# Two transformer layers on one core: probabilities become the stationary operand of the product with V

## The chip, the core and the metric

The kernel runs on 1 core of one Trainium2 chip. The metric is device time in microseconds (us) of one execution. The engines that matter are TensorE (PE; its weight loads are shown apart as PEld), VectorE (DVE), ScalarE (ACT), GpSimd (POOL) and the DMA queue of SyncE (SP). A matmul on TensorE loads a stationary operand (the weights, one column per output row) and then streams the moving operand through it, column by column, into PSUM. An fp32 product is issued as two passes, each with a load and a matmul, so the trace has two of each.

## What is computed

Two transformer layers over x of 16 batches x 128 tokens x 144 channels, both with 16 heads of 9 channels and a shift and scale taken from a condition; the first has a mixture of 4 experts as its MLP, the second a plain MLP of 576. The part that matters here is the same in both layers:

```python
attn = jax.nn.softmax(jnp.einsum('bhqd,bhkd->bhqk', q, k) * hd ** (-0.5), axis=-1)
o = jnp.einsum('bhqk,bhkd->bhqd', attn, v).transpose(0, 2, 1, 3).reshape(B, N, C)
o = o @ w_proj + b_proj
x = x + g_msa[:, None, :] * o
```

## The kernel before

Everything stays in SBUF between the stages; Q and K go once through a scratch in DRAM to be laid out by head. The order of the whole program is a generator, `program()`, whose steps every engine walks through, each issuing its own part; semaphores join them. Per layer there are 16 batches of 2 pairs; a *pair* here is a half of a batch's heads, 8 of 16. `attention_step(L, p)` emits the steps of pair p:

- `MAX` of pair p + 4 (`scores`, L1348, 8 bf16 matmuls into `s_pair`; VectorE then takes the row maxima, L1096, 1.22 us each), and for the first pair of a batch `MAX_T`, which turns the maxima of the next batch around (L1408) and stores them by a DMA as two extra rows of Q.
- `SCORE` of pair p (`scores_T`, L1370, 8 bf16 matmuls into `st_pair`, keys on partitions); ScalarE takes the exponential into `pr` (L824, 1.03 us). `pr` holds two pairs, keys on partitions, 128 queries per head, not normalised.
- `PROJ` of batch b - 2 in even pairs: two fp32 products (L1422, L1423), then VectorE adds the residual.
- `OUT_T` of batch b - 1 in odd pairs, see below.
- steps for the next group of four batches (normalising, transposing, QK and V products, splitting into bf16 parts, loads of Q and K), laid out over the pairs by `prep_order`.
- `PV` of pair p - 1 (`weigh`, L1389), and in odd pairs `ATT_T` of batch b - 1 (two transpositions of `an`, L1414 and L1415, then a copy to `aT`, L837).

The product with V has V as its stationary operand: for a head, 128 keys x 10 columns (9 channels and a column of ones, which gives the sum of the probabilities), and the head's 128 x 128 of `pr` streams. The result of head i lies on 10 partitions from 32 x (i mod 4), so four heads share the array by columns. It stands with channels on partitions, so it has to be turned: ScalarE copies a bank of 128 x 512 to `osb` (`o_out`, L831), TensorE transposes it in four pieces back into the bank (`out_T`, L1399), and then `normalise` on VectorE takes the reciprocal of the sums (L1111) and multiplies (L1114) into `an`. Banks 4 and 5 take turns by batch.

Of the kernel before, what the change touches and what calls it, by code (L numbers as in the profile page):

```python
# [12 lines left out]
P = 128  # L13
BATCH, SEQ, C = 16, 128, 144
HEADS, HD = 16, 9
# [30 lines left out]
def build(nc, x, cond, w_adaln, b_adaln, w_qkv, b_qkv, w_proj, b_proj, w_gate, w1, b1, w2, b2,  # L46
# [7 lines left out]
    with ExitStack() as ctx:  # L54
        def sb(name, shape, dt=F32):
            return ctx.enter_context(nc.sbuf_tensor(name, shape, dt))

        def sem(name):
# [108 lines left out]
        mT = sb("mT", [2 * HEADS, SEQ], BF16)  # L167
        pr = sb("pr", [P, 2, HP * SEQ])
        neg_one = pr[0:2, 0, 0:SEQ // 2].bitcast(BF16)
        osb = sb("osb", [P, 512])  # L170
        wp32, wr32 = resid[:, 0:2 * C], osb[:, 0:2 * C]
        first_resid = (resid, osb, pr[:, 1, 0:GT])
        later_resid = (resid, hid[:, 2 * HQ:2 * HQ + GT], hid[:, 2 * HQ + GT:2 * HQ + 2 * GT])
        rinv = sb("rinv", [P, HEADS])
        an = sb("an", [P, 2 * P])
# [21 lines left out]
            zeroed pooled neg_st silu cond_T cond_c mod_mm mod_T mod_done gate_c gate_st wsplit qk_weights split_s  # L197
            stats_s sums_s vars_s aggr_s rstd_s normed T_done h_main h_hi h_rest r_hi h_ready
            qk_mm part_a part_r part_b part_c scr_w v_mm v_ready
            padded s_mm max_s msplit mt_mm mt_c m_ld st_mm exp_s pv_mm o_ev o_T rinv_s an_s a_T a_c  # L200
            proj_mm att_t x_att g_att_ld0 g_att_ld1 g_mlp_ld gate_x cw_b mix_s mod_read
            gl_mm gl_c lg_T gate_s gate_e cw_s b2_s w1_mm gelu w2_mm acc_s acc_g x_mlp
            f1_mm f1_gelu f2_mm f2_t st_out""".split()
# [78 lines left out]
        def attention_step(L, p):  # L282

            B0, P0 = BATCH * L, NP * L
            b, h = p // PAIRS, p % PAIRS
            pre, first, mid, late = prep_order(L, p)
            yield from pre
            if p + LEAD < NP:
                yield "MAX", P0 + p + LEAD
            if h == 0 and 0 <= b + 1 < BATCH:  # L290
                yield "MAX_T", B0 + b + 1
            if 0 <= p:
                yield "SCORE", P0 + p
            yield from mid
            if h == 0 and 0 <= b - 2:
                yield "PROJ", B0 + b - 2
            if h == 1 and 0 <= b - 1:
                yield "OUT_T", B0 + b - 1
            yield from first
            yield from late  # L300
            if 0 <= p - 1:
                yield "PV", P0 + p - 1
            if h == 1 and 0 <= b - 1:
                yield "ATT_T", B0 + b - 1

        def attention_end(L):

            B1 = BATCH * (L + 1)
            yield "PV", NP * (L + 1) - 1
            yield "PROJ", B1 - 2  # L310
            yield "UP_PE", (L, 0, 2)
            yield "OUT_T", B1 - 1
            yield "GELU", (L, 0, 0)
            yield "UP_PE", (L, 0, 3)
            yield "ATT_T", B1 - 1
            yield "GELU", (L, 0, 1)
            yield "UP_PE", (L, 0, 4)
            yield "GELU", (L, 0, 2)
            yield "PROJ", B1 - 1
            yield "GELU", (L, 0, 3)  # L320
            yield "GELU", (L, 0, 4)
# [428 lines left out]
        def _(act):  # L750
# [72 lines left out]
                    act.wait_ge(s["part_c"], 3 * NG * (Pn // NP) + 6)  # L823
                sc.activation(pr[:, Pn % 2, :], st_pair[:, :], ACT.Exp, scale=SCALE).then_inc(s["exp_s"], 1)  # L824

            def o_out(B):
                need(act, "pv_mm", PAIRS * (B + 1))
                need(act, "o_T", B)
                if B % BATCH == 0:
                    act.wait_ge(s["part_c"], 3 * NG * (B // BATCH) + 6)  # L830
                sc.copy(osb[:, :], bank[O_BANK[B % 2]][:, :]).then_inc(s["o_ev"], 1)  # L831

            def a_out(B):
                o_bank = bank[O_BANK[B % 2]]
                need(act, "a_T", B + 1)
# [71 lines left out]
            for what, i in program():  # L907
                if what == "QK":
                    part_a(*i, QK_BANK[i[0]][i[1]])
                if what == "PART_B":  # L910
                    part_b(*i)
                if what == "V":
                    v_out(*i, V_BANK[i[0] % NG][i[1]])
                if what == "H_MAIN":
                    h_main(i)
                if what == "H_REST":
                    h_rest(i)
                if what == "H_SPLIT":
                    h_round(i)
                    rest_round(i)  # L920
                if what == "MAX_T":
                    m_out(i)
                if what == "SCORE":
                    exp_pair(i)
                if what == "PV" and i % PAIRS == PAIRS - 1:
                    o_out(i // PAIRS)
                if what == "ATT_T":
                    a_out(i)
                if what == "MOD":
                    mod_out(*i)  # L930
                if what == "ROUND_W":
                    round_weights(i)
                if what in ("UP", "GELU"):
                    gelu(*i)
                if what == "LOGITS":
                    logits_out(i)
                if what == "MIX":
                    act.wait_ge(s["gate_e"], i + 1)
                    sc.activation(ex[:, :, :], dl[:, :, :], ACT.Exp).then_inc(s["gate_x"], 1)
# [3 lines left out]
        def _(dve):  # L943
# [9 lines left out]
            def weights(L):  # L953

                dve.wait_ge(s["ld_qkv%d" % L], NQKV[L])
                need(dve, "part_c", 3 * NG * L)
                need(dve, "o_T", BATCH * L)
                for src, dst in ((sq[L], wp32), (sqr[L], wr32)):
                    sv = src[:, 0:2 * C].rearrange("p (w h d) -> p w d h", w=2, d=HD)
                    for w in range(2):  # L960
# [120 lines left out]
            def part_r(a, t, src):  # L1081
                n = rows(t)
                dve.wait_ge(s["part_a"], 3 * a + t + 1)
                if a % NG == 0 and t > 0:
                    need(dve, *(("o_T", BATCH * (a // NG)) if t == 1 else ("pv_mm", NP * (a // NG))))
                else:
                    need(dve, "part_c", 3 * (a - 1) + t + 1)
                v.tensor_tensor(by_batch(resid_of(a, t), n), by_batch(src, n), parts[0:n, t, :, 0, :],
# [17 lines left out]

            def normalise(B):
                o_bank = bank[O_BANK[B % 2]]
                need(dve, "o_T", B + 1)
                ov = o_bank[:, :].rearrange("p (h w) -> p h w", w=SLOT)  # L1110
                v.reciprocal(rinv[:, :], ov[:, :, HD]).then_inc(s["rinv_s"], 1)  # L1111
                dve.wait_ge(s["rinv_s"], B + 1)
                need(dve, "a_T", B)
# [93 lines left out]
            def setup():  # L1207
# [3 lines left out]
                v.memset(sqr[1][:, :], 0.0).then_inc(s["zeroed"], 1)  # L1211
                v.memset(c_nat[:, C:C + 1], 1.0)
                v.memset(hid4[64:65, :], 1.0)
                for i in O_BANK:
                    v.memset(bank[i], 0.0)
                v.memset(low_slots[:, :], 0.0)
                step(v.memset(mask[:, :], 0.0))
                for k in range(NS):
# [19 lines left out]
            for what, i in program():  # L1238
# [18 lines left out]
                    split_weights(i)  # L1257
                if what == "WEIGHTS":
                    weights(i)
                if what == "OUT_T":  # L1260
                    normalise(i)
                if what == "PROJ":
                    attention_residual(i)
# [13 lines left out]
        def _(pe):  # L1277
# [97 lines left out]
            def weigh(Pn):  # L1375
# [9 lines left out]
                    if B % BATCH == 0:  # L1385
                        need(pe, "part_r", 3 * a + 6)
                for i in range(HP):
                    c, q = i % NS, PAIRS * h + i // NS
                    last = te.matmul(bank[O_BANK[B % 2]][SLOT * c:SLOT * c + OW, q * SEQ:(q + 1) * SEQ],  # L1389
                                     V[:, G * (a % 2) + j, HP * h + i, :], pr[:, Pn % 2, i * SEQ:(i + 1) * SEQ],  # L1390
                                     start=True, stop=True)
                last.then_inc(s["pv_mm"], 1)

            def out_T(B):

                o_bank = bank[O_BANK[B % 2]]
                pe.wait_ge(s["o_ev"], B + 1)
                for q in range(4):
                    last = te.transpose(o_bank[:, q * SEQ:(q + 1) * SEQ], osb[:, q * SEQ:(q + 1) * SEQ],  # L1399
                                        ident[:, :])  # L1400
                last.then_inc(s["o_T"], 1)

            def max_T(B):
                pe.wait_ge(s["msplit"], 2 * B + 2)
# [124 lines left out]
            for what, i in program():  # L1529
# [13 lines left out]
                    scores_T(i)  # L1543
                if what == "PV":
                    weigh(i)
                if what == "OUT_T":
                    out_T(i)
                if what == "ATT_T":
                    att_T(i)
                if what == "PROJ":  # L1550
# [42 lines left out]
```

## Time and profile before

| | |
|---|---|
| median of 3 runs | 507.63 us (505.89 to 512.28) |
| profiled execution | 508.33 us, its span 506.4 us |
| busy, share of the span | PE 436.0 us (86%), PEld 349.7 (69%), DVE 303.4 (60%), ACT 276.4 (55%), POOL 88.9 (18%) |
| mean granted clock of TensorE | 0.926 |
| product with V, L1389 | 1024 passes, 43.8 us busy together |
| transpositions of `osb`, L1399 | 128, 21.5 us busy |
| copy to `osb`, L831 | 32, 589 ns each, 18.9 us |
| chain of work that ended last | PE 51%, DVE 15%, SPq 11%, DMA 10%, ACT 6% |

The profile is of one execution. Busy time of an engine is the union of its instructions; matmuls are pipelined and their ends modelled, so the distance from the start of one group to the start of the next tells more than its length. PEclk is the share of 2.4 GHz that was granted: 1.00 is 2.4 GHz, 0.50 is 1.2 GHz, and a mean between is a mixture of these two. In the first exponential (52.6 us) and the last of the first layer (162.6 us) the first attention has its ends, in those at 352.6 and 452.6 us the second. Between lies the expert MLP, after it the plain one.

### The profile page before, as it was taken

How to read it: one execution, taken by the hardware profiler on the slowest of the kernel's cores; microseconds unless marked ns; L12 is line 12 of the kernel's file. 1: busy time of each engine (PE TensorE's matmuls, PEld its weight loads, DVE VectorE, ACT ScalarE, POOL GpSimd, SP SyncE). 2: the span in 40 equal slices, each digit the busy share in tenths (PEclk: the TensorE clock that was granted, in tenths of full speed). 3: DMA queues.
4: the chain of work that ended last, by engine and by line, in shares of the span. 5: the costliest groups of instructions: out<-in, count | busy, mean ns of one | idle time of the engine just before them, and what ended most of it. 6: DMA issues, size and time to landing. Idle time of an engine off the chain costs nothing.

```text
span 506.4 us, 10608 instructions
## 1 busy us (share of the span) xinstructions
PE 436.0 (86%) x4010; PEld 349.7 (69%) x4010; DVE 303.4 (60%) x891; ACT 276.4 (55%) x523; POOL 88.9 (18%) x112
## 2 busy tenths in 40 slices
PE   4846888888889999999994999998898978888996
PEld 1415656666667779879873997797677767657775
DVE  7766576598874326368433362368777756754651
ACT  4642657776474590381174336613768754856552
POOL 3212001020000053045016200802020200000000
PEclk9877689799797999999998899998789997999999
DMA  7846536445431000000000115202435563210112
GB/s 217 248 133 180 155 97 165 142 129 132 125 91 27 1 1 2 25 0 1 24 1 0 28 44 168 68 0 67 137 99 154 152 152 121 69 31 1 49 48 70
DMA packets 51098, 42.49 MB, mean 84 GB/s; under 512 B 33287, under 2 KB 43454, under 8 KB 51044
## 3 DMA queue, kind: packets, MB, share of 16 engines
q1 hardware_dynamic: 51048, 41.82, 29.6%
q8 instruction: 32, 0.52, 0.4%
q14 instruction: 18, 0.15, 0.1%
HBM read 33.20 MB, written 8.29 MB: 82 GB/s over the span
## 4 chain that ended last, share of the span: by engine, by line
PE 51%; DVE 15%; SPq 11%; DMA 10%; ACT 6%; issue 5%; POOL 2%; DVEq 0%; ACTq 0%; POOLq 0%
PE bank L1507 14%; DVE mx L1096 4%; DMA KA<-qk_scratch 4%; PE s_pair L1348 4%; PE st_pair L1370 3%; SPq L617 3%; PE bank L1389 3%; PE bank L1525 3%; DMA qk_scratch<-parts 2%; PE bank L1293 2%; PE s_pair L1298 2%; PE s_pair L1299 2%; PE s_pair L1300 2%; PE st_pair L1298 2%; PE s_pair L1301 2%
## 5 line engine op out<-in xcount | busy, mean ns | idle before, releaser
L1096 DVE TENSOR_REDUCE mx<-s_pair 128x8 f32<-128x1024 f32 x64 | 78.2, 1221 | 35.9 <-PE s_pair L1348 35.3
L1507 PE MATMUL bank<-w_sb,hid 128*128 128x144 f32 x640 | 80.5, 286 | 0.9 <-DVE aT L1184 0.9
L1507 PEld LDWEIGHTS bank<-w_sb,hid 128*128 128x128 f32 x640 | 79.7, 190 | 1.9 <-DVE aT L1184 1.2
L824 ACT ACTIVATE pr<-st_pair 128x1024 f32<-128x1024 f32 x64 | 65.8, 1028 | 18.8 <-PE st_pair L1370 18.5
L873 ACT ACTIVATE hid<-s_pair 128x512 f32<-128x512 f32 x40 | 23.3, 612 | 51.4 <-PE s_pair L1301 51.4
L697 POOL TENSOR_TENSOR rstd<-var_eps,minus_half 128x4 f32<-128x4 f32 x16 | 16.2, 1012 | 175.8 <-DVE var_eps L1051 175.8
L1348 PE MATMUL s_pair<-KA,QA 81*128 81x128 bf16 x416 | 36.4, 238 | 12.1 <-DMA KA<-qk_scratch 8.1
L1389 PE MATMUL bank<-pr,V 128*10 128x128 f32 x1024 | 43.8, 293 | 0.0
L1348 PEld LDWEIGHTS s_pair<-KA,QA 81*128 81x128 bf16 x416 | 28.4, 107 | 21.5 <-issue 14.8
L1370 PE MATMUL st_pair<-QA,KA 83*128 83x128 bf16 x416 | 36.9, 240 | 5.5 <-DMA QA<-mT 5.2
L719 POOL TENSOR_TENSOR bw<-b_sb,cw 128x576 f32<-128x576 f32 x16 | 19.9, 1245 | 87.0 <-DVE cw L1167 87.0
L1370 PEld LDWEIGHTS st_pair<-QA,KA 83*128 83x128 bf16 x416 | 29.9, 109 | 7.0 <-issue 5.8
L1389 PEld LDWEIGHTS bank<-pr,V 128*10 128x10 f32 x1024 | 22.8, 95 | 16.5 <-issue 9.8
L1062 DVE TENSOR_SCALAR xn<-xs,mean,rstd 128x128 f32<-128x128 f32 x64 | 22.7, 354 | 10.1 <-POOL rstd L697 9.9
L1184 DVE SCALAR_TENSOR_TENSOR aT<-bank,cw,aT 128x144 f32<-128x144 f32 x48 | 17.6, 368 | 17.2 <-PE bank L1507 16.1
L763 ACT ACTIVATE h<-bank,b_main,a_main 128x128 f32<-128x128 f32 x64 | 24.0, 456 | 6.1 <-PE bank L1293 6.0
L837 ACT COPY aT<-bank 128x256 f32<-128x256 f32 x32 | 11.9, 373 | 27.9 <-PE bank L1415 27.8
L1399 PE MATMUL bank<-ident,osb 128*128 128x128 f32 x128 | 21.5, 294 | 4.5 <-ACT osb L831 4.3
L704 POOL TENSOR_TENSOR parts<-resid,parts 32x512 bf16<-32x512 f32 x8 | 9.2, 1150 | 91.9 <-ACT parts L799 91.9
L774 ACT ACTIVATE r<-bank,b_rest,a_rest 128x128 f32<-128x128 f32 x60 | 22.6, 465 | 4.0 <-PE bank L1293 3.9
L794 ACT CAST parts<-bank 128x512 bf16<-128x512 f32 (+1 forms) x18 | 10.4, 578 | 25.7 <-PE bank L1301 25.6
L873 ACT ACTIVATE hid<-st_pair 128x512 f32<-128x512 f32 x32 | 18.8, 611 | 8.2 <-PE st_pair L1301 8.2
(268 smaller groups left out, 947.8 us busy)
## 6 DMA issues: line engine op xcount, KB each, us to landing
QA<-qk_scratch SPq DMA_DIRECT2D x26, 324.0 KB
KA<-qk_scratch SPq DMA_DIRECT2D x78, 108.0 KB
qk_scratch<-parts SPq DMA_DIRECT2D x16, 384.0 KB, 4.0
g_att<-gate_scratch SPq DMA_DIRECT2D x16, 144.0 KB, 3.8
g_mlp<-gate_scratch SPq DMA_DIRECT2D x8, 288.0 KB, 3.5
hid<-qk_scratch SPq DMA_DIRECT2D x6, 324.0 KB
hid<-qk_scratch SPq DMA_DIRECT2D x18, 108.0 KB
hid<-in_L_cond_w SPq DMA_DIRECT2D x1, 1152.0 KB, 9.3
```

What stands on the lines that cost most here:

```text
L763: last = sc.activation(h32[:, j * SEQ:(j + 1) * SEQ], PREP[:, j * SEQ:(j + 1) * SEQ], ACT.Identity, bias=b_main[:, ph, t:t + 1], scale=a_m ...
L774: last = sc.activation(r32[:, j * SEQ:(j + 1) * SEQ], src[:, j * SEQ:(j + 1) * SEQ], ACT.Identity, bias=b_rest[:, ph, t:t + 1], scale=a_re ...
L824: sc.activation(pr[:, Pn % 2, :], st_pair[:, :], ACT.Exp, scale=SCALE).then_inc(s["exp_s"], 1)
L873: sc.activation(hid[:, m * GT:(m + 1) * GT], bank[m % 4][:, :], ACT.Gelu_apprx_tanh).then_inc(s["gelu"], 1)
L1062: v.tensor_scalar(xn[:, j, :], x_[:, 0:CM], mean[:, j:j + 1], rstd[:, j:j + 1], ALU.subtract, ALU.mult)
L1096: v.tensor_reduce(mx[:, HP * h:HP * (h + 1)], s_pair[:, :].rearrange("p (h k) -> p h k", k=SEQ), AX.X, ALU.max).then_inc(s["max_s"], 1)
L1298: te.matmul(dst, lo[:, cols], hhi[:, :], start=True, stop=False)
L1348: last = te.matmul(s_pair[:, i * SEQ:(i + 1) * SEQ], QAs[k][0:SROWS, HP * h + i, :], KAs[k][0:SROWS, HP * h + i, :], start=True, stop=True)
L1370: last = te.matmul(st_pair[:, i * SEQ:(i + 1) * SEQ], KAs[k][0:MROWS, HP * h + i, :], QAs[k][0:MROWS, HP * h + i, :], start=True, stop=True)
L1389: last = te.matmul(bank[O_BANK[B % 2]][SLOT * c:SLOT * c + OW, q * SEQ:(q + 1) * SEQ], V[:, G * (a % 2) + j, HP * h + i, :], pr[:, Pn % 2, ...
L1399: last = te.transpose(o_bank[:, q * SEQ:(q + 1) * SEQ], osb[:, q * SEQ:(q + 1) * SEQ], ident[:, :])
L1507: last = te.matmul(dst, hid[:, at:at + SEQ], w2_sb[:, MT1 * e + i, :], start=(i == 0), stop=(i == MT1 - 1))
```

## The change

In the product with V the operands change places. Stationary is now the head's 128 x 128 of `pr`, and the 10 columns of V stream. The result has queries on partitions and 16 x 10 columns for a batch's heads, as `normalise` wants it, so `o_out` and `out_T` are gone with `osb` and their semaphores. The first residual tile of the split of Q and K, which shared `osb`, is now a tile of its own, `resid1`. `normalise` waits for the product with V itself, and its step, now `NORM`, stands at the start of an odd pair's steps and not after its `PROJ`. Some waits that guarded `osb` go, and so do two memsets of the banks at the start.

```diff
--- before.py
+++ after.py
@@ -167,9 +167,9 @@
         mT = sb("mT", [2 * HEADS, SEQ], BF16)
         pr = sb("pr", [P, 2, HP * SEQ])
         neg_one = pr[0:2, 0, 0:SEQ // 2].bitcast(BF16)
-        osb = sb("osb", [P, 512])
-        wp32, wr32 = resid[:, 0:2 * C], osb[:, 0:2 * C]
-        first_resid = (resid, osb, pr[:, 1, 0:GT])
+        resid1 = sb("resid1", [P, GT])
+        wp32, wr32 = resid[:, 0:2 * C], resid1[:, 0:2 * C]
+        first_resid = (resid, resid1, pr[:, 1, 0:GT])
         later_resid = (resid, hid[:, 2 * HQ:2 * HQ + GT], hid[:, 2 * HQ + GT:2 * HQ + 2 * GT])
         rinv = sb("rinv", [P, HEADS])
         an = sb("an", [P, 2 * P])
...
@@ -285,6 +285,8 @@
             b, h = p // PAIRS, p % PAIRS
             pre, first, mid, late = prep_order(L, p)
             yield from pre
+            if h == 1 and 0 <= b - 1:
+                yield "NORM", B0 + b - 1
             if p + LEAD < NP:
                 yield "MAX", P0 + p + LEAD
             if h == 0 and 0 <= b + 1 < BATCH:
@@ -294,8 +296,6 @@
             yield from mid
             if h == 0 and 0 <= b - 2:
                 yield "PROJ", B0 + b - 2
-            if h == 1 and 0 <= b - 1:
-                yield "OUT_T", B0 + b - 1
             yield from first
             yield from late
             if 0 <= p - 1:
...
@@ -823,13 +823,6 @@
                     act.wait_ge(s["part_c"], 3 * NG * (Pn // NP) + 6)
                 sc.activation(pr[:, Pn % 2, :], st_pair[:, :], ACT.Exp, scale=SCALE).then_inc(s["exp_s"], 1)
 
-            def o_out(B):
-                need(act, "pv_mm", PAIRS * (B + 1))
-                need(act, "o_T", B)
-                if B % BATCH == 0:
-                    act.wait_ge(s["part_c"], 3 * NG * (B // BATCH) + 6)
-                sc.copy(osb[:, :], bank[O_BANK[B % 2]][:, :]).then_inc(s["o_ev"], 1)
-
             def a_out(B):
                 o_bank = bank[O_BANK[B % 2]]
                 need(act, "a_T", B + 1)
...
@@ -1081,8 +1071,8 @@
             def part_r(a, t, src):
                 n = rows(t)
                 dve.wait_ge(s["part_a"], 3 * a + t + 1)
-                if a % NG == 0 and t > 0:
-                    need(dve, *(("o_T", BATCH * (a // NG)) if t == 1 else ("pv_mm", NP * (a // NG))))
+                if a % NG == 0 and t == 2:
+                    need(dve, "pv_mm", NP * (a // NG))
                 else:
                     need(dve, "part_c", 3 * (a - 1) + t + 1)
                 v.tensor_tensor(by_batch(resid_of(a, t), n), by_batch(src, n), parts[0:n, t, :, 0, :],
@@ -1106,8 +1096,8 @@
 
             def normalise(B):
                 o_bank = bank[O_BANK[B % 2]]
-                need(dve, "o_T", B + 1)
-                ov = o_bank[:, :].rearrange("p (h w) -> p h w", w=SLOT)
+                dve.wait_ge(s["pv_mm"], PAIRS * (B + 1))
+                ov = o_bank[:, 0:HEADS * OW].rearrange("p (h w) -> p h w", w=OW)
                 v.reciprocal(rinv[:, :], ov[:, :, HD]).then_inc(s["rinv_s"], 1)
                 dve.wait_ge(s["rinv_s"], B + 1)
                 need(dve, "a_T", B)
@@ -1211,8 +1201,6 @@
                 v.memset(sqr[1][:, :], 0.0).then_inc(s["zeroed"], 1)
                 v.memset(c_nat[:, C:C + 1], 1.0)
                 v.memset(hid4[64:65, :], 1.0)
-                for i in O_BANK:
-                    v.memset(bank[i], 0.0)
                 v.memset(low_slots[:, :], 0.0)
                 step(v.memset(mask[:, :], 0.0))
                 for k in range(NS):
...
@@ -1385,20 +1373,10 @@
                     if B % BATCH == 0:
                         need(pe, "part_r", 3 * a + 6)
                 for i in range(HP):
-                    c, q = i % NS, PAIRS * h + i // NS
-                    last = te.matmul(bank[O_BANK[B % 2]][SLOT * c:SLOT * c + OW, q * SEQ:(q + 1) * SEQ],
-                                     V[:, G * (a % 2) + j, HP * h + i, :], pr[:, Pn % 2, i * SEQ:(i + 1) * SEQ],
-                                     start=True, stop=True)
+                    at = (HP * h + i) * OW
+                    last = te.matmul(bank[O_BANK[B % 2]][:, at:at + OW], pr[:, Pn % 2, i * SEQ:(i + 1) * SEQ],
+                                     V[:, G * (a % 2) + j, HP * h + i, :], start=True, stop=True)
                 last.then_inc(s["pv_mm"], 1)
-
-            def out_T(B):
-
-                o_bank = bank[O_BANK[B % 2]]
-                pe.wait_ge(s["o_ev"], B + 1)
-                for q in range(4):
-                    last = te.transpose(o_bank[:, q * SEQ:(q + 1) * SEQ], osb[:, q * SEQ:(q + 1) * SEQ],
-                                        ident[:, :])
-                last.then_inc(s["o_T"], 1)
 
             def max_T(B):
                 pe.wait_ge(s["msplit"], 2 * B + 2)
```

TensorE, the first whole batch of layer 0 from its second product with V on (`pr` and `V` are the operands of that product, `osb` and `an` those of the transpositions); first before:

```order
L1389 MATMUL bank<-pr,V 10x128 x8
L1348 MATMUL s_pair<-KA,QA 128x128 x8
L1370 MATMUL st_pair<-QA,KA 128x128 x8
L1399 MATMUL bank<-ident,osb 128x128 x4
L1389 MATMUL bank<-pr,V 10x128 x8
L1414 MATMUL bank<-ident,an 128x128
L1415 MATMUL bank<-ident,an 128x128
```

and the same place in the change:

```order
L1377 MATMUL bank<-V,pr 128x10 x8
L1336 MATMUL s_pair<-KA,QA 128x128 x8
L1358 MATMUL st_pair<-QA,KA 128x128 x8
L1377 MATMUL bank<-V,pr 128x10 x8
L1392 MATMUL bank<-ident,an 128x128
L1393 MATMUL bank<-ident,an 128x128
```

The four transpositions are gone; the product is 128 x 10 where it was 10 x 128; nothing else stands elsewhere on this engine.

VectorE at the first row maximum after a batch's product with V (`mx` is the maximum, `mp_pad` its two bf16 parts, `rinv` and `an` the output of `normalise`); first before:

```order
L1096 TENSOR_REDUCE mx<-s_pair 128x8
L1103 CAST mp_pad<-mx 128x16
L1105 TENSOR_TENSOR mp_pad<-mx,mp_pad 128x16
L1111 RECIPROCAL rinv<-bank 128x16
L1114 TENSOR_TENSOR an<-bank,rinv 128x144
L1072 TENSOR_TENSOR hlo<-h,hhi 128x512
```

and in the change:

```order
L1101 RECIPROCAL rinv<-bank 128x16
L1104 TENSOR_TENSOR an<-bank,rinv 128x144
L1086 TENSOR_REDUCE mx<-s_pair 128x8
L1093 CAST mp_pad<-mx 128x16
L1095 TENSOR_TENSOR mp_pad<-mx,mp_pad 128x16
L1062 TENSOR_TENSOR hlo<-h,hhi 128x512
```

The two instructions of `normalise` have moved ahead of the maximum and its split.

## Rows read from the trace of the kernel before

**Rows 1.** The granted clock of TensorE from the page, in 40 slices of the span.

```profile
PEclk9877689799797999999998899998789997999999
```

**Rows 2.** Stretches of both attentions: us, busy (x) per engine, PEclk, DMA share, GB/s.

```profile
52.60:162.60 110.00, 94.29 (x1174) 72.20 (x1172) 80.39 (x191) 72.58 (x133) 9.96 (x9) 0.86 0.44 119
352.60:452.60 100.00, 87.63 (x1178) 68.71 (x1177) 71.89 (x184) 67.14 (x122) 9.95 (x9) 0.91 0.42 119
```

**Rows 3.** Timeline of TensorE in two pairs: start us, us, engine, line, operation [idle before].

```profile
408.87 0.66 PE L1399 MATMUL bank<-ident,osb 128*128 128x128 f32 x4
409.46 0.62 PE L1389 MATMUL bank<-pr,V 128*10 128x128 f32 x16
410.60 0.33 PE L1414 MATMUL bank<-ident,an 128*128 128x128 f32 x1 [0.52 <-DVE an L1114]
...
410.88 0.61 PE L1348 MATMUL s_pair<-KA,QA 81*128 81x128 bf16 x8
...
411.39 0.61 PE L1370 MATMUL st_pair<-hid 83*128 83x128 bf16 x8
411.83 0.46 PE L1422 MATMUL bank<-wo_r,aT 128*128 128x144 f32 x2
...
412.47 0.63 PE L1389 MATMUL bank<-pr,V 128*10 128x128 f32 x16
413.03 0.62 PE L1348 MATMUL s_pair<-KA,QA 81*128 81x128 bf16 x8
```

**Rows 4.** Timeline of the same stretch, ScalarE's exponentials.

```profile
408.85 1.03 ACT L824 ACTIVATE pr<-st_pair 128x1024 f32<-128x1024 f32 x1
...
414.14 1.02 ACT L824 ACTIVATE pr<-st_pair 128x1024 f32<-128x1024 f32 x1 [0.39 <-PE st_pair L1370]
```

**Rows 5.** Weight loads (PEld) and matmuls: timeline rows, then lines with min/median/max ns.

```profile
411.78 0.30 PEld L1422 LDWEIGHTS bank<-wo_r,aT 128*128 128x128 f32 x2
412.47 0.34 PEld L1389 LDWEIGHTS bank<-pr,V 128*10 128x10 f32 x16
...
173.15 0.41 PE L1488 MATMUL bank<-ident,lgT 4*128 4x4 f32 x4
...
233.45 2.72 PE L1507 MATMUL bank<-w_sb,hid 128*128 128x144 f32 x20 [0.94 <-DVE aT L1184]
...
L1507 PEld LDWEIGHTS bank<-w_sb,hid x640: 186/190/192, 187.3 to 346.0; 128*128 128x128 f32 x160
L1507 PE MATMUL bank<-w_sb,hid x640: 283/286/390, 187.5 to 346.1; 128*128 128x144 f32 x160
...
L1488 PE MATMUL bank<-ident,lgT x16: 198/198/220, 173.2 to 309.7; 4*128 4x4 f32 x16
...
L1389 PEld LDWEIGHTS bank<-pr,V x1024: 87/92/143, 55.5 to 455.4; 128*10 128x10 f32 x171
```

**Rows 6.** Timeline of TensorE in a stretch at the lower clock.

```profile
419.07 1.01 PE L1348 MATMUL s_pair<-KA,QA 81*128 81x128 bf16 x8 [2.73 <-DMA KA<-qk_scratch]
...
420.83 0.79 PE L1422 MATMUL bank<-wo_r,aT 128*128 128x144 f32 x2
...
422.03 1.04 PE L1389 MATMUL bank<-pr,V 128*10 128x128 f32 x16
```

**Rows 7.** Two pairs of neighbouring stretches, columns as in Rows 2.

```profile
63.30:66.80 3.50, 2.09 (x25) 1.71 (x24) 2.38 (x4) 1.35 (x4) 0.00 (x0) 0.99 0.60 171
66.80:70.20 3.40, 3.40 (x31) 1.81 (x30) 2.19 (x8) 1.54 (x3) 0.00 (x0) 0.50 0.08 27
414.90:418.30 3.40, 0.64 (x10) 0.20 (x2) 0.84 (x5) 0.64 (x2) 0.00 (x0) 1.00 0.56 164
418.30:425.10 6.80, 6.03 (x55) 5.26 (x56) 3.71 (x8) 2.03 (x4) 0.00 (x0) 0.50 0.53 171
```

**Rows 8.** Timeline of TensorE over one QK product and the group after it.

```profile
102.46 0.48 PE L1298 MATMUL bank<-hhi,wqk_lo 128*128 128x512 f32 x1
...
103.57 0.63 PE L1389 MATMUL bank<-pr,V 128*10 128x128 f32 x16
```

More of the change, by code:

```diff
@@ L199, in build @@
             qk_mm part_a part_r part_b part_c scr_w v_mm v_ready
-            padded s_mm max_s msplit mt_mm mt_c m_ld st_mm exp_s pv_mm o_ev o_T rinv_s an_s a_T a_c
+            padded s_mm max_s msplit mt_mm mt_c m_ld st_mm exp_s pv_mm rinv_s an_s a_T a_c
             proj_mm att_t x_att g_att_ld0 g_att_ld1 g_mlp_ld gate_x cw_b mix_s mod_read
@@ L311, in attention_end @@
             yield "UP_PE", (L, 0, 2)
-            yield "OUT_T", B1 - 1
+            yield "NORM", B1 - 1
             yield "GELU", (L, 0, 0)
@@ L924, in _ @@
                     exp_pair(i)
-                if what == "PV" and i % PAIRS == PAIRS - 1:
-                    o_out(i // PAIRS)
                 if what == "ATT_T":
@@ L956, in weights @@
                 need(dve, "part_c", 3 * NG * L)
-                need(dve, "o_T", BATCH * L)
                 for src, dst in ((sq[L], wp32), (sqr[L], wr32)):
@@ L1259, in _ @@
                     weights(i)
-                if what == "OUT_T":
+                if what == "NORM":
                     normalise(i)
@@ L1545, in _ @@
                     weigh(i)
-                if what == "OUT_T":
-                    out_T(i)
                 if what == "ATT_T":
```

## The prediction

> **What bounds the kernel now.** I read first the stages. The two attention stretches take 110 and 100 us of the 506.4 us span, at a mean granted clock of 0.86 and 0.91 [rows 2]; the clock row of the page is at its lowest in these stretches and full in the expert part between them [rows 1]. Nothing outside them runs a changed instruction except the setup of VectorE, so the sum is made over these 210 us.
>
> Then I read TensorE's timeline in a quiet piece, two pairs of heads of one batch [rows 3]. Each row's distance to the next is what the group really occupies (the rows' lengths include the drain). From 410.88 to 413.03 there is no gap: scores and the small transposition 0.51, transposed scores 0.44, projection 0.64, product with V 0.56. The even pair is bound by TensorE's queue. The odd pair has the four transpositions of `osb` (0.59, 408.87 to 409.46), and then TensorE stands: the product with V is out of its way by about 410.0, the transposition of `an` starts only at 410.60, idle for 0.52 of it, since VectorE normalises after these transpositions. The two pairs together take 5.29 us from exponential to exponential [rows 4]. 32 batches of that are 169 us; the other 41 of the 210 are steps with QK or V products or transpositions for the next group between, waits for the loads of Q and K, and stretches at 1.2 GHz.
>
> **What the change removes.** The copy on ScalarE, the four transpositions (0.59 per batch) and the idle 0.52 behind them go. I count no gain for the copy itself: ScalarE is then waited for by nobody, because TensorE becomes much slower. The memsets of two banks at the start go too; I leave that at nothing (they can only shorten the start). `normalise` moves in VectorE's queue ahead of a row maximum, and now waits for the product with V directly. Queued behind it are that maximum, for which the next scores wait, but the maximum needs scores that stand behind the same product in TensorE's queue, so VectorE would wait anyway: nothing. If that cover were gone it would cost the reciprocal and product, about half a us a batch. No DMA is issued or moved.
>
> **What it adds: the weight loads.** A product of fp32 runs as two passes, each a load and a matmul (1024 for 512 heads). Before, a load has 10 columns and lasts 92 ns; 16 passes occupy 0.56 us with the change of array mode around them [rows 3, 5]. Now each of 16 passes loads 128 columns of fp32 and streams 10. The loads of this form last 190 ns, and the pair of them before the projection takes 0.30, so they follow each other at 0.30 - 0.19 = 0.11 us [rows 5]. Twenty passes of the expert product, 128 columns loaded and 144 streamed, take 2.72, so (2.72 - 0.29)/19 = 0.128 us each; there streaming may be what binds. So a pass costs 0.11 to 0.128; I take 0.115. The group is 16 x 0.115 = 1.84, and 0.10 more because the first load (190 against 92 ns) can't begin before the exponential is there: 1.94 us. The far lower bound is the transposition of logits, 128 columns loaded and 4 streamed: (0.41 - 0.20)/3 = 0.07 us; but it is one pass of another mode. The far upper one is twice 0.11, load and matmul not overlapping at all: 0.22.
>
> *At 2.4 GHz.* One batch: 0.51 + 0.44 + 0.64 for the even pair, 0.45 + 0.45 + 0.28 for the odd one (0.28 is 410.60 to 410.88), 2 x 1.94 for V: 2.77 + 3.88 = 6.65 us against 5.29. No other engine is near that. 32 batches are 213 us. 22 steps carry QK, V or early MLP products, at 1.1 us as between 102.46 and 103.57 [rows 8]; V's are shorter, so 1.0 on average, 22. 12 steps carry four transpositions, 0.5 each, 6. The last four pairs of a layer have no scores, -4. Waits for loads shrink, since a batch gives them 1.4 us more; I leave 5. Sum 242 us, against 210: +32.
>
> *At 1.2 GHz.* Here I expect the larger part. The product with V streamed all 128 columns of the probabilities; now it streams 10 and spends its time loading. Of a batch's 6.65 us, columns stream in about 4 x 0.44 (scores), 0.5 (projection), 0.2 (transpositions) and 0.3: 2.8 us, 41%; before, with 0.4 for the transpositions and 0.8 for V, 3.7 of 5.29, 69%. What the clock does is seen in pairs of stretches [rows 7]. In 63.30 to 66.80 TensorE was busy for 2.09 of 3.5 us, with two waits for DMAs in it, and the next stretch was granted 0.50. In 414.90 to 418.30 it stood for a load, 0.64 busy, and 418.30 to 425.10 ran at 0.50, although TensorE was busy 6.03 of 6.80 there. At 0.50 everything is as slow as the row 420.83 to 422.03 says, 1.20 for the projection that took 0.64 [rows 6]. A TensorE that is the bound and runs at half the clock streams half as many columns a us, which keeps it there: before, it had slack at 2.4 GHz and dense work at 1.2 and came back; now it hasn't. Both layers' attention begins beside such stretches.
>
> The price, with everything doubled: even pair without V 2.96 (419.07 to 422.03 [rows 6]), odd one 2 x 1.18 = 2.36, V 16 x 0.23 + 0.1 = 3.78 each. A batch is 12.9, 32 of them 412; the extra products 2 x 28 = 56; no scores at the end, -7: 461 us, +251, which gives 759. Not all of it will be at 1.2 GHz: the stretch 66.80 to 70.20, at 0.50 itself, had a QK product in it and no wait [rows 7], and the clock must have risen soon after it, since the page's slice 63.3 to 76.0, the sixth, still reads 0.8 [rows 1]. I let half of the 22 steps with such products run at 2.4 GHz, each 12.9/2 + 2.0 - (6.65/2 + 1.0) = 4.1 us shorter: -45. That half is a choice, between none (759) and all attention (540). So 508.3 + 251 - 45 = **714 us**. The profiled execution took 508.3 (span 506.4, the rest lies around it), the median of the runs 507.6, so no correction.
>
> The Trainium skill, TensorE: Matmul & The Clock Gate, section LDWEIGHTS, gives a load as its columns / 1.2 GHz, 107 ns for 128; the 0.11 of the trace agrees. The Trainium skill, TensorEngine Tiling, section Performance Considerations, advises for 32 or fewer moving columns to swap the operands and tile by columns, which is the kernel before: it speaks against this change, as the sum does.
>
> **The rivals.**
> 1. *The clock stays as it is (chance 0.27).* Loads may keep the clock up as streaming does; nothing in before separates them, since where 128 columns are loaded long streams run too. Then +32: 540 us, and 10 more for each 0.01 a pass (64 x 16 x 0.01), to 553 at 0.128.
> 2. *Not slower (0.08).* TensorE's pass costs 0.07, as in the logits' transposition. V is 16 x 0.07 + 0.1 = 1.22, a batch 2.77 + 2.44 = 5.21; in all 32 x 5.21 + 24 = 191, plus 13 of waits for loads that then stay: 204, so -6, 502 us. It decides from 0.07 us a pass downward. If a pass cost what the 10-column loads do, (0.34 - 0.09)/15 = 0.02 [rows 5], V would be 16 x 0.02 + 0.1 = 0.42, a batch 3.6, and VectorE and ScalarE would bind before that: under 498, chance 0.02 of the 0.08. Against both: fp32 loads of 128 columns last 190 ns wherever two passes are made, and follow 0.11 apart. The Trainium skill, TensorE: Matmul & The Clock Gate, section Back-to-back issue gap, has one price, about 25 ns, for any matmul of 1 to 64 columns, without its load; it is on the side of this rival.
> 3. *Slower still (0.07).* Loads overlap nothing, 0.22 a pass: 64 x 16 x 0.105 = 108 us more at 2.4 GHz (648), twice that at 1.2 (over 900).
> 4. *Mostly at 1.2 GHz (0.58)*: my forecast, its own range 650 to 765.
>
> **Numbers.** Range 535 to 765: it leaves out rival 2 and most of rival 3, and holds the rest. About 2% is what a measurement here can tell from no change. Faster by over 2% needs a pass under 0.06: 0.02. Within 2%: 0.06. Slower: 0.92.
>
> **What would show it.** The group of the product with V: 16 loads of 190 ns, 0.11 to 0.12 apart (0.22 to 0.24 at 0.50). No rows of `osb`; `an` ready long before its transposition. ScalarE and VectorE waiting for TensorE in every pair. Granted clock of the attention stretches near 0.5 to 0.6 where it was 0.86 and 0.91; if it is above 0.8, my main step is wrong and the time is near 540. If loads stand 0.07 apart or less, the whole argument falls.

## The result

The changed kernel takes 618.25 us, median of 6 runs (614.86 to 628.92), where the kernel before takes 506.79 (6 runs, 505.57 to 512.28): 1.219 times as long, 95% interval 1.2135 to 1.225. The sign was forecast, and the mechanism; the size was not: 714 us was predicted, 206 us more than before, and 111 came.

The profile is of one execution, the slowest of the six (628.92 us, span 627.1), so it is compared below with the profiled execution of the kernel before (span 506.4), 121 us shorter. Its page, in the rows that answer to those of before: busy time, and the granted clock in 40 slices [rows 1].

```profile
PE 586.0 (93%) x3882; PEld 533.9 (85%) x3882; DVE 302.2 (48%) x889; ACT 260.5 (42%) x491; POOL 89.8 (14%) x112
...
PEclk9866567885555579999997999956969555555999
...
L1377 PEld LDWEIGHTS bank<-V,pr 128*128 128x128 f32 x1024 | 189.6, 282 | 2.7 <-issue 0.5
L1377 PE MATMUL bank<-V,pr 128*128 128x10 f32 x1024 | 184.6, 321 | 0.0
```

The weight loads of the product with V alone fill 189.6 us. The two attentions, again from the first exponential of a layer to its last, by stretches (us, busy of PE, PEld, DVE, ACT, POOL, granted clock, DMA):

```profile
51.20:214.90 163.70, 163.41 (x1119) 159.25 (x1117) 80.68 (x194) 65.37 (x117) 10.83 (x9) 0.60 0.31 81
411.50:565.90 154.40, 154.40 (x1122) 150.99 (x1122) 74.36 (x187) 59.90 (x107) 9.93 (x9) 0.64 0.28 77
```

They were 110 and 100 us at 0.86 and 0.91 [rows 2]; now 163.7 and 154.4 at 0.60 and 0.64. That is 108 of the 121 us between the two profiled executions. Behind both attentions the same low clock runs on, to 228.6 and 580.1 us, and there most of the rest lies. TensorE is busy in 163.41 of the 163.7 us and in all of the 154.4; it is the one bound.

A batch in the part without extra products, timeline of TensorE (start, length, line, operation). It answers to [rows 3]:

```profile
495.94 3.53 PE L1377 MATMUL bank<-V,pr 128*128 128x10 f32 x16
499.32 0.45 PE L1392 MATMUL bank<-ident,an 128*128 128x128 f32 x1
...
499.78 1.06 PE L1336 MATMUL s_pair<-KA,QA 81*128 81x128 bf16 x8
500.63 0.31 PE L1386 MATMUL bank<-identb,mp_pad 128*128 128x128 bf16 x1
500.74 1.06 PE L1358 MATMUL st_pair<-QA,KA 83*128 83x128 bf16 x8
501.59 0.79 PE L1400 MATMUL bank<-wo_r,aT 128*128 128x144 f32 x2
...
502.66 3.43 PE L1377 MATMUL bank<-V,pr 128*128 128x10 f32 x16
505.93 1.01 PE L1336 MATMUL s_pair<-KA,QA 81*128 81x128 bf16 x8
...
507.59 1.61 PE L1377 MATMUL bank<-V,pr 128*128 128x10 f32 x7
```

Not one row waits. From 495.94 to 507.59 is 11.65 us for the batch (the kernel before took 5.29, at 2.4 GHz [rows 4]), 6.65 of them in two groups of the product with V (3.38 and 3.27, at 1.2 GHz). The same group at 2.4 GHz, in a stretch that had it:

```profile
99.03 1.85 PE L1377 MATMUL bank<-V,pr 128*128 128x10 f32 x16
100.74 0.31 PE L1392 MATMUL bank<-ident,an 128*128 128x128 f32 x1
```

1.71 us. A matmul of the group lasts 0.17 at the least, so a pass costs (1.85 - 0.17)/15 = 0.112 us at 2.4 GHz, and (3.43 - 0.37)/15 = 0.204 at 1.2. What the clock did, by stretches:

```profile
51.10:88.60 37.50, 37.21 (x216) 35.12 (x213) 16.00 (x39) 14.73 (x27) 3.31 (x3) 0.50 0.36 94
88.60:102.30 13.70, 13.70 (x154) 13.52 (x155) 8.33 (x19) 7.92 (x17) 1.16 (x1) 1.00 0.65 154
102.30:115.90 13.60, 13.60 (x80) 13.31 (x80) 6.76 (x13) 7.33 (x14) 0.00 (x0) 0.50 0.33 102
115.90:136.40 20.50, 20.50 (x213) 19.73 (x211) 15.92 (x32) 13.21 (x23) 4.35 (x3) 1.00 0.48 115
136.40:228.60 92.20, 92.20 (x516) 90.10 (x516) 34.75 (x98) 25.45 (x44) 2.01 (x2) 0.50 0.16 43
```

Two things are to be seen. The clock is at 1.2 GHz while PE is busy for the whole stretch, and for up to 92 us on end; in the kernel before, both falls shown followed waits [rows 7], and here TensorE ran without a gap through the one at 136.40. And the rise at 88.60 came right behind a QK product, four matmuls that stream 512 columns each (the last two are shown):

```profile
87.44 0.63 PE L1288 MATMUL bank<-hR,wqk_r 128*128 128x512 f32 x1
87.87 0.63 PE L1289 MATMUL bank<-hhi,wqk_hi 128*128 128x512 f32 x1
88.30 2.01 PE L1377 MATMUL bank<-V,pr 128*128 128x10 f32 x16
```

The rises at 115.9, 433.4 and 467.5 us also fall inside or right behind a QK product, the one at 457.2 does not; and behind the QK product that ended at 79.98 the clock stayed down. So such a product goes before most of the rises, but it doesn't always bring one.

### The profile page after: what moved, and what is told of

The parts are those of the page before. It is cut to its first block, busy times and chain, and to the rows that moved or that the text cites. A ratio compares the mean times of both kernels' runs of the same rounds, so it can differ in the third digit from the quotient of the medians.

```text
span 627.1 us, 10304 instructions
## 1 busy us (share of the span) xinstructions
PE 586.0 (93%) x3882; PEld 533.9 (85%) x3882; DVE 302.2 (48%) x889; ACT 260.5 (42%) x491; POOL 89.8 (14%) x112
## 4 chain that ended last, share of the span: by engine, by line
PE 82%; SPq 5%; DVE 3%; ACT 3%; DMA 2%; POOL 2%; issue 1%; DVEq 0%; ACTq 0%; POOLq 0%
PE bank L1377 27%; PE bank L1485 12%; PE st_pair L1358 7%; PE s_pair L1336 6%; PE bank L1400 3%; PE bank L1281 2%; PE bank L1401 2%; PE bank L1503 2%; PE s_pair L1286 2%; PE st_pair L1286 2%; PE s_pair L1287 2%; PE s_pair L1288 2%; PE s_pair L1289 2%; SPq L617 1%; PE st_pair L1287 1%
## 5 line engine op out<-in xcount | busy, mean ns | idle before, releaser
L1377 PEld LDWEIGHTS bank<-V,pr 128*128 128x128 f32 x1024 | 189.6, 282 | 2.7 <-issue 0.5
L1377 PE MATMUL bank<-V,pr 128*128 128x10 f32 x1024 | 184.6, 321 | 0.0
L824 ACT ACTIVATE pr<-st_pair 128x1024 f32<-128x1024 f32 x64 | 65.5, 1024 | 107.7 <-PE st_pair L1358 107.7
L1336 PE MATMUL s_pair<-KA,QA 81*128 81x128 bf16 x416 | 44.0, 270 | 6.6 <-DVE mx L1086 3.5
L1358 PE MATMUL st_pair<-QA,KA 83*128 83x128 bf16 x416 | 47.3, 282 | 2.6 <-DMA QA<-mT 2.3
L1336 PEld LDWEIGHTS s_pair<-KA,QA 81*128 81x128 bf16 x416 | 38.9, 131 | 9.8 <-DVE mx L1086 5.9
L1358 PEld LDWEIGHTS st_pair<-QA,KA 83*128 83x128 bf16 x416 | 39.7, 133 | 3.2 <-issue 2.5
L1114 DVE TENSOR_TENSOR tmp<-bank,g_att 128x144 f32<-128x144 f32 x32 | 9.8, 305 | 63.9 <-PE bank L1401 63.9
L704 POOL TENSOR_TENSOR parts<-resid,parts 32x512 bf16<-32x512 f32 (+1 forms) x12 | 14.1, 1174 | 126.8 <-ACT parts L799 126.8
L1101 DVE RECIPROCAL rinv<-bank 128x16 f32<-128x16 f32 x32 | 8.2, 256 | 45.6 <-PE bank L1377 45.6
L1286 PE MATMUL bank<-hhi,wqk_lo 128*128 128x512 f32 (+1 forms) x18 | 11.2, 622 | 12.4 <-DVE hR L1068 12.4
```

Of the source, the lines that this page charges most:

```text
L1286: te.matmul(dst, lo[:, cols], hhi[:, :], start=True, stop=False)
L1336: last = te.matmul(s_pair[:, i * SEQ:(i + 1) * SEQ], QAs[k][0:SROWS, HP * h + i, :], KAs[k][0:SROWS, HP * h + i, :], start=True, stop=True)
L1358: last = te.matmul(st_pair[:, i * SEQ:(i + 1) * SEQ], KAs[k][0:MROWS, HP * h + i, :], QAs[k][0:MROWS, HP * h + i, :], start=True, stop=True)
L1377: last = te.matmul(bank[O_BANK[B % 2]][:, at:at + OW], pr[:, Pn % 2, i * SEQ:(i + 1) * SEQ], V[:, G * (a % 2) + j, HP * h + i, :], start=T ...
```

## Experiments on the clock

Is the low clock the cost, and do the thin streams cause it? The same loads, in the same places, with more columns streamed beside them tell.

**More columns, 120.**

```diff
-                    last = te.matmul(bank[O_BANK[B % 2]][:, at:at + OW], pr[:, Pn % 2, i * SEQ:(i + 1) * SEQ],
-                                     V[:, G * (a % 2) + j, HP * h + i, :], start=True, stop=True)
+                    dst = bank[O_BANK[B % 2]][:, at:at + 12 * OW].rearrange("p (r w) -> p r w", w=OW)
+                    last = te.matmul(dst, pr[:, Pn % 2, i * SEQ:(i + 1) * SEQ],
+                                     V[:, G * (a % 2) + j, HP * h + i, :].unsqueeze(1).to_broadcast([P, 12, OW]),
+                                     start=True, stop=True)
```

> The changed kernel, but each product with V streams its head's 10 columns twelve times over: 120 columns to the same place and the 110 behind it, which the next heads then overwrite with their own results. The output is the same. Streaming 120 columns of fp32 should take 240 cycles, 0.10 us at 2.4 GHz, and lie beside the next load (0.112 us a pass in the changed kernel). Theory A (the clock falls because TensorE streams too little while it loads): granted clock of the attention stretches back above 0.95, the 16 passes still 1.8 us, time about 540 us. Theory B (the clock falls for another reason, or loads alone count for nothing and nothing else helps): clock 0.62 to 0.66 in attention as before, time 618 us. Theory C (a stream and the next load don't overlap): passes of 0.2 us, time above 618.

Measured: 516.24 us (4 runs, 515.7 to 518.6), 1.0196 times the kernel before, interval 1.0165 to 1.0226. Its attentions, by stretches, and a batch of its timeline:

```profile
53.50:163.40 109.90, 107.67 (x1119) 104.39 (x1117) 79.32 (x194) 65.03 (x118) 10.82 (x9) 0.97 0.45 119
355.00:462.00 107.00, 106.90 (x1122) 104.53 (x1122) 73.66 (x187) 59.90 (x106) 9.92 (x9) 0.98 0.40 111
```

```profile
424.03 2.00 PE L1378 MATMUL bank<-V,pr 128*128 128x120 f32 x16
425.86 0.27 PE L1394 MATMUL bank<-ident,an 128*128 128x128 f32 x1
...
427.04 0.47 PE L1402 MATMUL bank<-wo_r,aT 128*128 128x144 f32 x2
427.34 0.41 PE L1403 MATMUL bank<-wo_m,aT 128*128 128x144 f32 x2
427.58 1.94 PE L1378 MATMUL bank<-V,pr 128*128 128x120 f32 x16
429.36 0.61 PE L1336 MATMUL s_pair<-KA,QA 81*128 81x128 bf16 x8
429.81 0.61 PE L1358 MATMUL st_pair<-QA,KA 83*128 83x128 bf16 x8
430.26 0.99 PE L1378 MATMUL bank<-V,pr 128*128 128x120 f32 x7
```

Twelve times the streaming in this product makes the kernel 102 us faster. It does the same loads; the granted clock of attention is 0.97 and 0.98. The group takes 1.83 and 1.78 us, a little more than 1.71: a stream of 120 columns stays beside the loads. Theory A holds, B and C fall; its time, 540 us, was 24 too high, for the reasons given below. A batch takes 6.23 us (424.03 to 430.26).

**30 and 60 columns**, the same edit with 3 and 6 in place of 12.

> The same with the 10 columns streamed three times over, 30 columns. Theory A: part of the way, attention's granted clock 0.7 to 0.9, 570 to 605 us. Theory B: 618. Theory C: passes 0.02 us longer, 640.

> The changed kernel with the 10 columns of each product streamed six times over, 60 columns. 10 columns gave 618 us, 30 gave 592 to 620, 120 gave 516. Theory A (the clock follows what TensorE streams): the stream of 60 stays hidden beside the load, so passes 0.112 us; granted clock in attention above 0.9, 516 to 535 us. Rival (120 columns helped because TensorE's passes become as long as a load, so that it never stands between them): at 60 half of each pass is still empty, clock and time stay near those of 30 columns, 590 or more.

| columns streamed a pass | time, us | of before | granted clock, first and second attention |
|---|---|---|---|
| 10 (the change) | 618.25 (614.9 to 628.9) | 1.219 | 0.60, 0.64 |
| 30 | 611.66 (591.9 to 619.8) | about 1.21, no interval | 0.69, 0.66 |
| 60 | 531.91 (526.5 to 543.3) | 1.049 (1.039 to 1.059) | 0.86, 0.90 |
| 120 | 516.24 (515.7 to 518.6) | 1.020 (1.017 to 1.023) | 0.97, 0.98 |

The clocks are those of one execution each, from the first exponential of a layer to its last, with 30 columns and then with 60:

```profile
51.50:198.70 147.20, 145.80 (x1120) 142.14 (x1117) 80.45 (x194) 65.15 (x117) 10.88 (x9) 0.69 0.34 90
395.80:547.30 151.50, 151.50 (x1123) 147.82 (x1123) 74.42 (x187) 60.12 (x107) 9.95 (x9) 0.66 0.28 79
```

```profile
50.10:172.50 122.40, 120.20 (x1119) 116.18 (x1120) 82.65 (x195) 64.95 (x117) 10.05 (x9) 0.86 0.42 108
364.00:477.90 113.90, 113.71 (x1123) 110.80 (x1123) 73.83 (x187) 59.97 (x106) 9.95 (x9) 0.90 0.37 105
```

At 60 a pass is still about half empty of streaming (an estimate: 144 columns take 0.128 us a pass [rows 5], so 60 take 0.05 of the 0.112), the group takes 1.72 us (424.02 to 425.74), and most of the clock is back: the rival named there falls. The time lies in the range that I gave; the clock of 0.86 and 0.90 is a little below the 0.9. With 30 I expected 570 to 605 us and a clock of 0.7 to 0.9, and got more time and less clock, with runs further apart than those of any other kernel here. What the chip counts, the columns that stream or the results that they write, these runs don't part: both grow together.

**The type, bf16.** Probabilities and V of this product in bf16 (rounding differs there).

```diff
-        V = sb("V", [P, 2 * G, HEADS, OW])
+        V = sb("V", [P, 2 * G, HEADS, OW], BF16)
+        pb = sb("pb", [P, 2, HP * SEQ], BF16)
...
-                sc.activation(pr[:, Pn % 2, :], st_pair[:, :], ACT.Exp, scale=SCALE).then_inc(s["exp_s"], 1)
+                sc.activation(pb[:, Pn % 2, :], st_pair[:, :], ACT.Exp, scale=SCALE).then_inc(s["exp_s"], 1)
...
-                    last = te.matmul(bank[O_BANK[B % 2]][:, at:at + OW], pr[:, Pn % 2, i * SEQ:(i + 1) * SEQ],
+                    last = te.matmul(bank[O_BANK[B % 2]][:, at:at + OW], pb[:, Pn % 2, i * SEQ:(i + 1) * SEQ],
```

> The changed kernel with the probabilities and V in bf16 for this product: one pass of each instead of two, and loads of 128 columns of bf16, which last 98 ns and pace at 0.056 us for the scores. The rounding of this product is what differs. Theory A (the fp32 loads are the price): the 8 passes take 0.45 to 0.6 us a pair, time 480 to 495 us, below before. Rival (the swap costs by its number of loads or by its thin streams, whatever the type): the clock stays low in attention, 550 or more.

Measured: 504.46 us (10 runs, 502.1 to 509.6), 0.999 of before (0.9946 to 1.0036). So the swap without the fp32 loads costs nothing, and it doesn't gain the 12 us and more that I expected either. Its timeline shows the group at the low clock, and who is waited for:

```profile
422.90 0.40 PE L1378 MATMUL bank<-V,pb 128*128 128x10 bf16 x8
423.16 1.01 PE L1337 MATMUL s_pair<-KA,QA 81*128 81x128 bf16 x8
...
426.59 1.03 PE L1337 MATMUL s_pair<-hid 81*128 81x128 bf16 x8 [0.57 <-DVE mx L1087]
```

The eight passes occupy 0.26 us even at 1.2 GHz. The granted clock of its attentions was 0.77 and 0.73 (50.6 to 158.1 and 345.4 to 447.9 us), where before it was 0.86 and 0.91 [rows 2], and TensorE was busy 163.6 of these 210 us, where it had been 181.9. Against my expectation, both theories are wrong in a part: the low clock is there, and the time isn't. TensorE now waits for VectorE and for loads; how much of the missing gain is the low clock and how much the waits, no run separates.

## Experiments on what was removed, and what took its place

**Without the turn.** The kernel before, without copy and transpositions, the rest in its old order. The normalising step reads the unturned layout, and a scaled copy of the sums stands for their reciprocal, so values behind it differ.

```diff
-                if what == "PV" and i % PAIRS == PAIRS - 1:
-                    o_out(i // PAIRS)
...
-                need(dve, "o_T", B + 1)
+                dve.wait_ge(s["pv_mm"], PAIRS * (B + 1))
...
-                v.reciprocal(rinv[:, :], ov[:, :, HD]).then_inc(s["rinv_s"], 1)
+                v.tensor_scalar(rinv[:, :], ov[:, :, HD], 0.001, 1.0, ALU.mult, ALU.add).then_inc(s["rinv_s"], 1)
...
-                if what == "OUT_T":
-                    out_T(i)
```

> The kernel before with the copy to osb and the four transpositions left out; the normalising step reads the bank as the product leaves it, and a scaled copy of the sums stands where their reciprocal stood, so what comes behind attention is computed from other values. It measures what the change removes, apart from what it adds. Theory A (my sum): a plain batch falls from 5.29 us towards 4.2, where VectorE binds, less the waits for loads that then grow: 485 to 492 us. Rival: the removed work is hidden behind waits for Q and K: 505 us.

Measured: 506.66 us (10 runs), 0.9985 of before (0.9946 to 1.0025). The removal alone is worth nothing that shows; the 485 to 492 of my theory A were wrong, and the rival had the number, for a part of the reason. Its waits (who waited for whom, us in total, times, longest), and below them the same two of the kernel before:

```profile
PE bank L1411 <- DVE an L1111: 25.5, 26, 2.5
PE s_pair L1345 <- DMA KA<-qk_scratch: 10.9, 7, 2.8
```

```profile
PE bank L1414 <- DVE an L1114: 11.5, 15, 2.0
PE s_pair L1348 <- DMA KA<-qk_scratch: 8.1, 6, 2.7
```

TensorE comes to the transposition of `an` earlier and waits there longer: `normalise` still stands behind the row maximum on VectorE. The clock has a share too: it was granted 0.82 and 0.90 in the two attentions (0.86 and 0.91 before), and of the 18.9 us of transpositions only 10.5 are missing from TensorE's busy time (171.4 us against 181.9); its idle time there grew by 12.4.

**Without the turn, and with the move.** The same, with `normalise` moved ahead of the row maximum as the change has it.

```diff
+            if h == 1 and 0 <= b - 1:
+                yield "OUT_T", B0 + b - 1
             if p + LEAD < NP:
                 yield "MAX", P0 + p + LEAD
...
-            if h == 1 and 0 <= b - 1:
-                yield "OUT_T", B0 + b - 1
```

> The kernel before without the copy and the transpositions, as in before_no_turn (the normalising step works on the untuned layout, so later values differ), and the normalising step moved ahead of the row maximum in VectorE's queue as the change has it. In before_no_turn TensorE waited 25 to 33 us for an, longer than before. Theory A (the turn's removal is only worth something with the move): the wait for an goes, plain batches near 4.3 us, and what remains is waits for loads of Q and K: 493 to 500 us. Theory B (loads bound the attention as a whole already): no change, 505 us, all of the wait for an turned into waits for loads.

Measured: 502.56 us (10 runs), 0.9934 of before (0.9885 to 0.9983): the gain is there but small, and below what I expected (493 to 500). The wait for `an` is gone from the longest waits, and this stands in its place (timeline of TensorE, and its waits):

```profile
407.96 0.33 PE L1411 MATMUL bank<-ident,an 128*128 128x128 f32 x1
408.12 0.27 PE L1412 MATMUL bank<-ident,an 128*128 128x128 f32 x1
413.51 1.01 PE L1345 MATMUL s_pair<-KA,QA 81*128 81x128 bf16 x8 [5.11 <-DMA KA<-qk_scratch]
```

```profile
PE s_pair L1345 <- DMA KA<-qk_scratch: 17.8, 5, 5.1
PE s_pair L1345 <- DMA hid<-qk_scratch: 7.0, 2, 4.4
```

24.8 us of waits for the loads of Q and K (`hid` holds the fifth slot of both), in seven places, against 10.2 in before. Behind such a wait the clock is low: the scores after it last 1.01 where they lasted 0.62.

**Light loads**, in two kernels: a slot that was filled before in its layer gets 4 of 16 heads, so later batches compute on old heads. The load of K is edited in the same way.

```diff
-                sp.dma_start(QAs[k][0:SROWS, :, :].rearrange("p h t -> p (h t)"),
...
+                H = HEADS if B % BATCH < RING else 4
+                sp.dma_start(QAs[k][0:SROWS, 0:H, :].rearrange("p h t -> p (h t)"),
...
```

> The kernel before with the light loads alone (later batches compute on old heads). If waits for loads, with the stretches at 1.2 GHz behind them, cost the kernel before its 8 to 20 us: 487 to 497 us, granted clock in attention above 0.95. If they are not what stalls it: 505.

> The same, and the loads of Q and K to a slot that was filled before in its layer bring a quarter of their heads, 4 of 16 (later batches compute on old heads; the output differs). Same number of DMAs, a quarter of the bytes. If loads are what takes the place of the removed work: 475 to 485 us. If not: as no_turn_early.

Measured: 498.04 us (4 runs), 0.988 of before (0.982 to 0.993), with the turn still in it; 494.8 us (4 runs), 0.978 (0.970 to 0.987), without turn and with the move. Both gain, the first just above its upper bound of 497, the second less than the 475 to 485 expected. So the bytes of these loads are a part of what bounds attention: 8 us in either kernel. But removal and move together are worth 3 us with light loads (498.04 to 494.8) and 3 with full ones (505.89 to 502.56), so it isn't these bytes that swallow the removed work. With light loads 15 us of waits for Q and K remain in the second kernel, so something in the way to these DMAs other than their bytes is late; and in the profiled executions the clock falls with the removal, from 0.88 and 0.97 in the two attentions to 0.84 and 0.88 (I had expected above 0.95 for the first kernel). What causes either isn't taken apart.

**The same lightening in stream120.**

> stream120 with the light loads of before_light (a slot filled before in its layer gets 4 of 16 heads; later batches compute on old heads, the output differs). In stream120 a plain batch takes 6.23 us and only 4.5 us of waits for K are left. If its fp32 weight loads now bound it and swallow the waits for Q and K: 511 to 516 us, where the same lightening took 8 us from the kernel before. If DMAs still bind: 505 to 508 us, the 8 us again.

Measured: 514.37 us (4 runs, 511.8 to 516.9), 1.022 of before (1.015 to 1.029), where stream120 was at 1.020: no difference that these runs settle, as expected; before lost 8 us with the same edit. The fp32 weight loads bound that kernel, and most waits for Q and K lie under them. This is why the groups, 64 x (1.78 - 0.56) = 78 us more of TensorE's time less 32 x 0.59 = 19 for the transpositions, show as only 10 at 2.4 GHz. The other 49 are found in the stretches of the two attentions: TensorE's idle time fell from 28.1 us to 2.3; what the low clock added (an estimate, the length of each stretch times 1 less its granted clock) fell from 24 to 5; and the projection is 0.10 shorter in each of 32 batches.

**The move, in stream120**, undone (`normalise` back behind the maximum).

> stream120 with the normalising step put back behind the row maximum in VectorE's queue. My prediction counted the move at nothing. In stream120 TensorE is the bound, 1.8 us of passes lie between the row maximum's scores and the transposition of an, and VectorE has its 1.2 us maximum and the normalising 0.6 in that time: 516 to 518 us, no change. Rival (the move matters, as before_no_turn suggests): the transposition of an waits 0.3 to 1 us per batch, 525 to 545 us.

Measured: 517.91 us (4 runs), 1.027 of before (1.022 to 1.033), against 1.020 (1.017 to 1.023) for stream120. The intervals overlap; the medians differ by 1.7 us, the ratios by 0.8%, so the move is worth 2 to 4 us here if anything. That is where TensorE is the bound; where it isn't, no_turn_early at 0.993 (0.989 to 0.998) against before_no_turn at 0.9985 (0.995 to 1.003) points to half a per cent, and doesn't settle it either.

## Why the prediction was right in kind and too large

- **The loads.** Predicted 0.115 us a pass, 1.94 a group at 2.4 GHz; measured 0.112, and 1.71 to 1.83 a group. The choice of the nearer row was right; the far lower bound, 0.07 from the transposition of the logits, doesn't hold for this product. The load sets the pass and not the stream: a group takes about the same with 10, 60 and 120 columns (1.71, 1.72, 1.78). The 0.10 for the first load isn't to be seen. At 1.2 GHz I took 3.78 a group; it is 3.27 to 3.38.
- **A batch at 2.4 GHz.** Predicted 6.65, measured 6.23 (stream120). The groups are 0.27 of that. The projection takes 0.54 and not 0.64: in the kernel before, the next row starts 0.33 to 0.34 us after L1423 where it is the product with V in its four column parts, and 0.24 to 0.25 where it is a transposition or the product that computes V (L1332); now it is 0.24 to 0.25 in front of the product with V too. I had copied the row with that difference in it.
- **At 2.4 GHz in all.** Predicted +32, measured +10 (stream120). Stream120's two attentions take 216.9 us where my sum had 242. 13 us of that are the 0.42 of 32 batches. The rest: 32 batches of 6.23 are 199, which leaves 18 us for all extra products and waits, where I had added 29 (22 + 6 - 4 + 5). Which of these four terms was how much too high isn't worked out.
- **The clock.** The step that speaks of it was right: at 10 columns the clock falls and stays, 102 of the 111 us are it (618.25 less 516.24), and giving the streams back gives the time back. I had put the low clock at 174 us (251 - 45 - 32). Its size failed in three terms. A batch at 1.2 GHz takes 11.65, not 12.9, which is 40 us over 32 batches: 0.91 of the 1.25 are the two groups (3.38 and 3.27, where I had 3.78 each), 0.13 the projection (1.07 and not 1.20). The extra products, too high as said above, I had doubled with the rest. And I let half of the 22 steps with QK, V or early MLP products run at 2.4 GHz, 48 us in all, and called that a choice; the trace has about 16 of the 22 there, with 3 of the 12 transposition steps, and 78.5 us at 2.4 GHz in the two attentions, since the clock, once risen, stayed up over the V steps.
- **What is removed.** I counted 0.59 and 0.52 a batch as gone, and they are gone, but nearly all of it would have been given back, as waits for loads and for `an` and as a lower clock, had nothing been added (before_no_turn, no_turn_early). In my sum this made no error, as the added work covers it; as a reading of the kernel before it was wrong to take the removed work for time won: less work on TensorE brought more waits and a lower clock.
- **The move of `normalise`** at nothing: right as far as the runs can tell (a difference of 2 to 4 us, not settled).
- **The rivals.** Rival 1, the clock stays, is false, and its 540 was too high as well. Rivals 2 and 3 fell with the row of the loads, 0.112 us apart and not 0.07 or 0.22. Of the things that would show the steps, the loads of 190 ns, 0.11 apart at 2.4 GHz, and the waits of ScalarE and VectorE for TensorE are there (107.7 us for the exponentials, 18.5 before); the clock of 0.60 and 0.64 is at and above the upper end of the 0.5 to 0.6 that I named. That the time came within the range owes something to its width: it reached from the price of rival 1 to a clock that never rises.

## What to carry to other kernels

Before making a large operand stationary for the sake of the result's layout, count its loads at the pace of the kernel's own loads of that width and type: an fp32 one of 128 columns cost 0.11 us a pass here at 2.4 GHz and 0.20 at 1.2, and two passes a product, with 10 columns streamed as with 120. Then look at how much of the bound engine's time streams columns, not at how busy it is: a TensorE that mostly loads can lose half its clock, and here, where it was the bound, it stood there for up to 92 us on end. With 60 columns beside each load most of the clock was back. Work taken off such a kernel is only worth what the next late thing, here loads, a queue position and the clock itself, leaves of it, so measure the removal alone before crediting it.

## What the runs showed of the hardware that I had not expected

- The granted clock stood at 0.50 for 92 us on end with TensorE 100% busy by its rows, and its weight loads busy 98% of that time. Streaming each head's 10 columns twelve times, into places that are overwritten, made the kernel 102 us faster. The Trainium skill, TensorE: Matmul & The Clock Gate, Part 1, tells of a clock that falls when the engine idles; here a fall at 136.40 us followed no idle time.
- A load of 128 fp32 columns follows the clock: passes of 0.112 and 0.204 us, loads that last from 187 ns at 2.4 GHz to 337 at 1.2 (min, median and max of all 1024, most of them at 1.2):

```profile
L1377 PEld LDWEIGHTS bank<-V,pr x1024: 187/333/337, 53.8 to 574.2; 128*128 128x128 f32 x171
L1377 PE MATMUL bank<-V,pr x1024: 172/366/368, 54.0 to 574.3; 128*128 128x10 f32 x171
```

- A load of 128 bf16 columns with 10 streamed is no bound: eight in 0.26 us at the lower clock.
